# A two-part convolution, attention and expert kernel: three more rounds of expert weights and three token pieces are loaded before the first part ends

## The chip, the cores and the metric

One Trainium2 chip, one of its cores. The metric is the time of one execution on the device in microseconds (us); lower is better. All tensors are float32.

## The reference

The input is 8 images of 128 channels and 56 x 56 points (3136 points, called tokens later).

1. Deformable convolution: the group-normalised image gives 18 offsets a point; nine taps are gathered at the shifted places, weighted, and multiplied by `conv_w`; the input is added.
2. Attention: each image's 3136 tokens are normalised, then causal attention with one head of 128, added to the tokens (`t2` below).
3. Experts, which the change is about. Cut to what matters:

```python
logits = einsum('bsd,ed->bse', x, gate_w) + gate_b        # x: normalised tokens, 64 experts
probs = softmax(logits, axis=1)                            # over the tokens
topv, topi = the 8 largest tokens of each expert
pooled = sum over the 8 of topv * x[topi]                  # [8 images, 64 experts, 128]
h = gelu([pooled, 1] @ weight1[e])                         # 129 x 512 for each expert
out = [h, 1] @ weight2[e]                                  # 513 x 128 for each expert
outputs[topi] += out * topv
```

## The kernel before, in words

The kernel is two programs, one after the other, each of five engines that wait for each other by semaphores; a barrier of all engines stands between them.

**First part** (`first_part`, L328). It goes through 8 x 25 = 200 tiles of 128 tokens (`ALL` = 200), as a pipeline of steps written out by hand: in step `s` tile `s` is sampled and convolved, tile `s - 6` gets its scores, tile `s - 7` its probabilities and attention, tile `s - 8` (`LAG_T` = 8) its result `t2`, which SP stores four tiles at a time in `t2_dram` (L525). Small work (`MISC`) is hung on the steps: the logits of the gate (L669), and, 9 to 14 steps into the next image, the eight largest logits, the exponentials, the sparse probabilities (`logit` after that), the sum `rz`, and `pooled` (L921). SP stores the probabilities in `pm_dram` (L544, semaphore `pm_out`) and the sums in `rz_dram` (L545, semaphore `rz_out`). For the last image there are no more tiles beside this: steps 200 to 214 only finish it. This stretch is called the drain.

SP's queue runs in program order, its waits included. On it are the stores, the token loads, and the first expert weights: round 0 in the seventh image, rounds 1 to 3 at step `ALL + 1`, once the last convolution is done, because `shared`, where these weights go, holds the padded image and the gathered taps until then. At the end SP waits for the three late loads, for all stores of probabilities and sums, and for the token stores; then comes the barrier.

**Second part** (`second_part`, L1297). 64 experts in 16 rounds of four (`ROUNDS` = 16, `EXPERTS` = 4). A round needs 1024 KB of first weights and 1024 KB of second weights, in a ring of four slots (`WSLOTS`) in `shared`. Beside it the token pieces: each image's `t2` comes back from `t2_dram` in two pieces (16 in all, by POOL into three `stage` buffers), is turned by TensorE (L1543, seven units of up to 512 tokens an image) and kept in `res`, 8 x 3136 columns, by VectorE (even units, L1455) and ScalarE (odd units, L1425).

TensorE's order for each `k` from 0 to 18 is: first product of round `k` (L1507); placing of the outputs of round `k - 3` (L1552); the first two units of piece `k`; the turning of round `k - 1`'s hidden values (L1516); the rest of the units; second product of round `k - 2` (L1527). SP's order for each `k` is: wait until round `k - 2`'s first product frees the slot, load the first weights of round `k + 2`; wait for round `k - 4`'s second product, load the second weights of round `k`. POOL loads piece `k` when piece `k - 3` has been turned.

When all rounds are placed, VectorE scales the outputs by `rz` (L1486), TensorE multiplies them with the stored probabilities (L1584, 56 products, seven or eight banks ahead), VectorE adds each to `res` (L1496), and ScalarE's queue stores `res` in 16 pieces (12.85 MB). The probabilities of the first two images come through the `stage` buffers, of the others through `shared`.

## Time and profile before

| what | value |
|---|---|
| three runs | 2759.89, 2761.46, 2781.64 us |
| median | 2761.46 us |
| the profiled execution, its time | 2761.01 us |
| the profiled execution, its span | 2759.0 us |
| mean granted clock of TensorE | 0.975 of full |
| TensorE busy | 2556.5 us, 93% of the span |
| DMA, mean over the span | 139 GB/s |

The span is the time from the first to the last recorded event of the profiled execution; the execution's own time is 2.0 us longer. The shares are means over both parts, which differ: the first part ends near 2609 us, and the second takes the remaining 150 us. Times below count from the span's start. "SPq", "POOLq" and "ACTq" are the queues on which these engines issue DMAs; the time of such a row is that of the issue, not of the transfer.

### The profile page before, as it was taken

To read this page: it belongs to the slowest core of one execution; us is meant where nothing else is said; L and a number is where in the kernel's file an instruction comes from. 1 tells how busy PE (TensorE), PEld (TensorE's weight loads), DVE (VectorE), ACT (ScalarE), POOL (GpSimd) and SP (SyncE) were. 2 spreads that over 40 slices of the span, in tenths; PEclk is the share of its full clock that TensorE was granted. 3 is DMA by queue.
4 is the path that set the end of the run, shared out by engine and by line. 5 is a ranking of instruction groups with operands and counts; after the bars stand their busy time and mean duration, and the time that the engine had idled before them with its cause. 6 is when DMAs were issued, how large, how long until landed. Compare 5 with 4: busy or idle time off the path is not lost. (4 is left out here: it accounts for less than half of the span.)

```text
span 2759.0 us, 53901 instructions
## 1 busy us (share of the span) xinstructions
PE 2556.5 (93%) x19262; PEld 2042.3 (74%) x19262; DVE 1890.7 (69%) x7300; ACT 1777.5 (64%) x4144; POOL 1768.3 (64%) x1831
## 2 busy tenths in 40 slices
PE   4688999999999999999999999999999998999687
PEld 3466787777877787778877787778877887777564
DVE  4457767876687766876687777867688767765435
ACT  3456767667776767766776767666776767665330
POOL 4777776777577766777577766777577766740000
PEclk8799999999999999999999999999999999999899
DMA  6354434643356334643266334734364333432299
GB/s 188 112 159 135 117 113 128 159 131 113 91 168 148 115 104 127 162 121 113 87 176 146 113 101 130 173 108 121 92 165 150 112 103 111 120 80 96 68 397 395
DMA packets 218150, 382.63 MB, mean 139 GB/s; under 512 B 43786, under 2 KB 128714, under 8 KB 216988
## 3 DMA queue, kind: packets, MB, share of 16 engines
q0 software_dynamic: 88992, 250.76, 32.3%
q1 hardware_dynamic: 126299, 113.98, 13.9%
q10 hardware_dynamic: 2592, 14.45, 1.3%
q8 instruction: 154, 2.52, 0.4%
q14 instruction: 113, 0.92, 0.1%
HBM read 316.92 MB, written 62.13 MB: 137 GB/s over the span
## 5 line engine op out<-in xcount | busy, mean ns | idle before, releaser
L592 POOL DMA_INDIRECT shared<-pair_table,idx x1800 | 1747.8, 971 | 700.1 <-issue 537.0
L1250 PEld LDWEIGHTS bank_o<-vals,prob_t 128*128 128x128 f32 x4800 | 584.5, 192 | 120.6 <-ACT prob_t L639 65.0
L1250 PE MATMUL bank_o<-vals,prob_t 128*128 128x128 f32 x4800 | 613.0, 277 | 35.9 <-ACT prob_t L639 35.9
L639 ACT ACTIVATE prob_t<-bank_r 128x512 f32<-128x512 f32 (+2 forms) x704 | 369.6, 546 | 415.7 <-PE bank_r L1236 414.0
L889 DVE SCALAR_TENSOR_TENSOR shared<-shared,wb 128x128 f32<-128x128 f32 x1800 | 514.8, 347 | 167.9 <-ACT shared L620 166.8
L901 DVE CUSTOM_DVE_ANT_0 prob<-bank_r,mask 128x512 f32<-128x512 f32 (+2 forms) x704 | 429.0, 624 | 249.3 <-PE bank_r L1227 231.0
L620 ACT ACTIVATE shared<-shared,wa 128x128 f32<-128x128 f32 x1800 | 560.3, 391 | 60.1 <-DMA shared<-pair_table,idx 59.0
L1227 PE MATMUL bank_r<-keys,qt 128*128 128x512 f32 (+3 forms) x1344 | 587.9, 554 | 0.7 <-ACT qt L662 0.3
L1209 PE MATMUL bank_r<-convw_t,smp_t 128*128 128x128 f32 x3600 | 478.5, 279 | 8.7 <-ACT smp_t L625 8.7
L1209 PEld LDWEIGHTS bank_r<-convw_t,smp_t 128*128 128x128 f32 x3600 | 443.6, 195 | 49.6 <-ACT smp_t L625 28.0
L1236 PE MATMUL bank_r<-ident,prob 128*128 128x128 f32 x2504 | 367.0, 273 | 4.1 <-ACT prob L721 3.9
L1227 PEld LDWEIGHTS bank_r<-keys,qt 128*128 128x128 f32 x1344 | 228.7, 193 | 143.5 <-issue 141.1
L721 ACT ACTIVATE prob<-prob,nmax 128x1664 f32<-128x1664 f32 (+23 forms) x200 | 325.3, 1626 | 13.8 <-DVE nmax L1019 12.5
L1201 PE MATMUL bank_r<-ident,shared 128*128 128x128 f32 x1800 | 262.0, 286 | 73.1 <-DVE shared L889 73.0
L1236 PEld LDWEIGHTS bank_r<-ident,prob 128*128 128x128 f32 x2504 | 291.8, 141 | 19.2 <-issue 12.7
L1201 PEld LDWEIGHTS bank_r<-ident,shared 128*128 128x128 f32 x1800 | 208.8, 146 | 109.3 <-DVE shared L889 99.0
L625 ACT ACTIVATE smp_t<-bank_r 128x384 f32<-128x384 f32 x600 | 248.8, 484 | 11.8 <-PE bank_r L1201 10.9
L1005 DVE TENSOR_TENSOR t<-bank_r,t 128x128 f32<-128x128 f32 x200 | 57.1, 286 | 154.1 <-PE bank_r L1209 154.1
L934 DVE SCALAR_TENSOR_TENSOR t<-bank_o,inv_total,t 128x128 f32<-128x128 f32 x192 | 67.3, 350 | 51.4 <-PE bank_o L1250 39.8
L1370 POOL MEMSET pooled_t<- 128x1024 f32 x1 | 1.0, 952 | 151.5 <-POOLq L330 151.5
L1111 PE MATMUL bank_r<-shared,offw_t 128*32 128x448 f32 x896 | 98.0, 554 | 0.0
L1132 PEld LDWEIGHTS bank_r<-wv_t,keys 128*128 128x128 f32 x400 | 54.7, 197 | 29.5 <-issue 29.5
(189 smaller groups left out, 2260.2 us busy)
## 6 DMA issues: line engine op xcount, KB each, us to landing
shared<-in_dram SPq DMA_DIRECT2D x32, 1024.0 KB, 17.9
shared<-pair_table,idx POOLq DMA_INDIRECT x1800
pair_table<-rows_out SPq DMA_DIRECT2D x112, 256.0 KB
t<-in_dram SPq DMA_DIRECT2D x48, 256.0 KB
t_dram<-t SPq DMA_DIRECT2D x48, 256.0 KB
shared<-in_dram SPq DMA_DIRECT2D x7, 1568.0 KB, 14.8
stage<-t_dram POOLq DMA_DIRECT2D x8, 832.0 KB, 7.4
pm_dram<-logit SPq DMA_DIRECT2D x8, 800.0 KB, 6.6
```

Source lines behind the costliest of these rows:

```text
L592: pool.indirect_dma_start(g[t % RING][:, n, :], None, pair_table[b % 2], bass.IndirectOffsetOnAxis(ap=idx[:, b % 2, i * TAPS + n:i * TAPS ...
L620: last = act.activation(first, first, ACT.Copy, scale=wa[:, b % 2, i * TAPS + n:i * TAPS + n + 1])
L625: act.activation(smp_t[p][:], ring_bank(("smp", t, p))[:, 0:3 * P], ACT.Copy).then_inc(smp_ev, 1)
L639: act.activation(prob_t[q % 3][:, 0:w], ring_bank(("prob", t, c))[:, 0:w], ACT.Copy)\
L721: act.activation(row, row, ACT.Exp, bias=nmax[r][:, 0:1], accum_out=total[r][:, 0:1])\
L889: last = dve.scalar_tensor_tensor(first, g[t % RING][:, n, C:], wb[:, b % 2, i * TAPS + n:i * TAPS + n + 1], first, ALU.mult, ALU.add)
L901: dve.tensor_tensor_reduce(prob_at(t, k0, w), ring_bank(("score", t, c))[:, 0:w], m, 1.0, NEG, ALU.add, ALU.max, cmax[t % 2][:, c:c + 1]). ...
L1201: last = pe.transpose(bank[:, n * P:(n + 1) * P], g[step % RING][:, 3 * p + n, 0:C], ident[:])
L1209: last = pe.matmul(ring_bank(("conv", step, 0))[:, 0:P], smp_t[p][:, n % 3 * P:(n % 3 + 1) * P], convw_t[:, n, :], start=(n == 0), stop=(n ...
L1227: last = pe.matmul(bank[:, 0:w], qt[k % 2][:, at:at + P], key_chunk(tb, k0, w), start=True, stop=True)
L1236: last = pe.transpose(ring_bank(use)[:, n * P:(n + 1) * P], prob_at(v, k0 + n * P, P), ident[:])
L1250: last = pe.matmul(attn_ps, prob_t[q % 3][:, n * P:(n + 1) * P], vals[:, slot(tb, at), :], start=(at == 0), stop=(at == ti))
```

## The change

The large buffers of the second part, `res` and the three `stage` buffers, are now allocated before the first part, and most of the first part's tiles (`prob`, `t1`, `rows_out`, `xf`, `logit`, `keys`, `vals` in `res`; `convw_t`, `qt`, `prob_t`, `xf_t`, two of `smp_t` in `stages`) are cut out of them. Before, both parts' tiles lay over each other by the allocator's choice.

Three more weight slots lie in `res`: two where `keys` and `vals` are, one over `t1`, `rows_out` and the end of `prob`. Round 0 uses the last of the seven; rounds 1 to 4 use the four of `shared` and are loaded where 0 to 3 were; rounds 5 and 6 use the other two. Rounds 0, 5 and 6 are loaded by SP at step `ALL + LAG_T`, when the last attention is done and the last `t2` is made. From round 7 on the ring is the four slots of `shared`.

POOL loads token pieces 0, 1 and 2 at the end of its first part: when the last convolution and attention are done, and the third also when the last logits have been multiplied.

SP no longer waits at the end of the first part for the late loads, the probabilities and the sums. In the second part ScalarE waits for `pm_out` ahead of its first copy, VectorE for `late_in` and `pm_out`, POOL and SP for `pm_out` ahead of their loads of probabilities, and SP waits for `rz_out` at `k` = 7 and loads the sums there.

```diff
-EXPERTS, WSLOTS = 4, 4
+EXPERTS, WSLOTS, MORE_SLOTS = 4, 4, 3
+STAGES = 3
 WHALF = EXPERTS * HID
 NEG = -3.0e38
 EPS = 1e-5
 RSQRT_GUESS = float(0x5f3759df)
 MIDDLE = 12 * P
 PROB_COLS = 48 * P
+STAGE_COLS = NP - GPI // 2 * CHUNK
+MORE_AT = [B * N - 4 * WHALF, B * N - 2 * WHALF, PROB_COLS + T1_GROUPS * PER * C + 2 * ROW_GROUP * C - 2 * WHALF]
+FIRST_LOADS = WSLOTS + MORE_SLOTS
 END = ALL + 16
 
 
@@ -301,23 +305,47 @@
...
+def expert_slots(shared, res):
 
     halves = [shared[:, h * WHALF:(h + 1) * WHALF] for h in range(2 * WSLOTS)]
+    halves += [res[:, at + h * WHALF:at + (h + 1) * WHALF] for at in MORE_AT for h in range(2)]
     return ([h.rearrange("p (e h) -> p e h", e=EXPERTS) for h in halves[0::2]],
...
-def load_experts(sp, k, which, w1, w2, shared, w_in):
-
-    r, at = k % WSLOTS, slice(k * EXPERTS, (k + 1) * EXPERTS)
-    w1s, w2s = expert_slots(shared)
+def expert_slot(k):
+
+    if k == 0:
+        return FIRST_LOADS - 1
+    return k - 1 if k < FIRST_LOADS else (k - FIRST_LOADS) % WSLOTS
+
+
+def loads_of_slot(k):
+
+    return sum(expert_slot(u) == expert_slot(k) for u in range(k + 1))
+
+
+def slot_user_before(k):
+
+    return max(u for u in range(k) if expert_slot(u) == expert_slot(k))
+
...
+def load_experts(sp, k, which, w1, w2, slots, w_in):
+
+    r, at = expert_slot(k), slice(k * EXPERTS, (k + 1) * EXPERTS)
+    w1s, w2s = slots
...
+def load_stage(pool, k, stage, t2_dram, stage_in):
+
+    b, h = divmod(k, 2)
+    n0, n1 = (0, GPI // 2 * PER) if h == 0 else (GPI // 2 * PER, TILES)
+    pool.dma_start(stage[k % STAGES][:, 0:(n1 - n0) * C].rearrange("p (t c) -> p t c", c=C),
+                   t2_dram[b][:, n0:n1, :]).then_inc(stage_in[k % STAGES], 16)
...
+        stage = [stages[:, r * STAGE_COLS:(r + 1) * STAGE_COLS] for r in range(STAGES)]
+        at_res, at_stages = [0], [0]
+
+        def part(of, at, cols):
+            at[0] += cols
+            return of[:, at[0] - cols:at[0]]
...
-        convw_t = sb("convw_t", [P, TAPS, P])
+        convw_t = part(stages, at_stages, TAPS * P).rearrange("p (n o) -> p n o", o=P)
...
-        smp_t = [sb(f"smp_t{p}", [P, 3 * P]) for p in range(PIECES)]
-        rows_out = [sb(f"rows_out{r}", [P, ROW_GROUP, C]) for r in range(2)]
-        t1 = sb("t1", [P, T1_GROUPS * PER, C])
         bn_a, mv_a = sb("bn_a", [P, 6]), sb("mv_a", [P, T1_GROUPS * PER, 2])
...
-        keys = sb("keys", [P, SLOTS * P])
-        vals = sb("vals", [P, SLOTS, P])
-        qt = [sb(f"qt{r}", [P, CHUNK]) for r in range(2)]
-        prob = sb("prob", [P, PROB_COLS])
+        prob = part(res, at_res, PROB_COLS)
+        t1 = part(res, at_res, T1_GROUPS * PER * C).rearrange("p (s c) -> p s c", c=C)
+        rows_out = [part(res, at_res, ROW_GROUP * C).rearrange("p (i c) -> p i c", c=C) for r in range(2)]
+        assert MORE_AT[2] >= MIDDLE + N and MORE_AT[2] + 2 * WHALF == at_res[0]
+        xf = part(res, at_res, SLOTS * C).rearrange("p (s c) -> p s c", c=C)
+        logit = part(res, at_res, NP)[0:E, :]
+        smp_t = [part(of, at, 3 * P) for of, at in ((res, at_res), (stages, at_stages), (stages, at_stages))]
+        keys = part(res, at_res, SLOTS * P)
+        vals = part(res, at_res, SLOTS * P).rearrange("p (s c) -> p s c", c=P)
+        assert at_res[0] == B * N and B * N - 2 * SLOTS * P == MORE_AT[0]
+        qt = [part(stages, at_stages, CHUNK) for r in range(2)]
+        prob_t = [part(stages, at_stages, CHUNK) for r in range(3)]
+        xf_t = part(stages, at_stages, CHUNK)
+        assert at_stages[0] <= STAGES * STAGE_COLS
...
+                if step == ALL + LAG_T:
+
+                    after(attended, ALL)
+                    after(t2_done, ALL)
+                    for k in (0, WSLOTS + 1, WSLOTS + 2):
+                        for which in (1, 2):
+                            load_experts(sp, k, which, w1, w2, slots, w_in)
...
@@ -548,7 +599,7 @@
                     filled(after, ("chunk", B - 1, OFF_CHUNKS - 1))
                     after(rows_ev, ROW_GROUPS * B)
                     for which in (1, 2):
-                        load_experts(sp, 0, which, w1, w2, shared, w_in)
+                        load_experts(sp, 1, which, w1, w2, slots, w_in)
                 if step == (B - 1) * TILES + 20:
 
                     after(indexed, B)
@@ -558,12 +609,9 @@
                 if step == ALL + 1:
 
                     after(conv_done, ALL)
-                    for k in range(1, WSLOTS):
+                    for k in range(2, WSLOTS + 1):
                         for which in (1, 2):
-                            load_experts(sp, k, which, w1, w2, shared, w_in)
-            after(late_in, 16 * 3)
-            for done in (pm_out, rz_out):
-                after(done, 16 * B)
+                            load_experts(sp, k, which, w1, w2, slots, w_in)
...
+            for k in range(STAGES):
+
+                for r in range(2):
+                    after(t2_out[r], 16 * len(range(r, GPI * (k // 2 + 1), 2)))
+                after(conv_done, ALL)
+                after(attended, ALL)
+                if k == STAGES - 1:
+                    filled(after, ("logit", B - 1, GPI - 1))
+                load_stage(pool, k, stage, t2_dram, stage_in)
...
-        res = sb("res", [P, B, N])
-        w1s, w2s = expert_slots(shared)
-        stage = [sb(f"stage{r}", [P, NP - HALF * CHUNK]) for r in range(STAGES)]
+        res = res[:].rearrange("p (b n) -> p b n", n=N)
+        w1s, w2s = slots
+        stage = [stages[:, r * STAGE_COLS:(r + 1) * STAGE_COLS] for r in range(STAGES)]
...
-            for k in range(TURN_PIECES):
-                if k >= STAGES:
-                    pool.wait_ge(res_tp, units_of(k - STAGES)[-1] + 1)
-                b, h = divmod(k, 2)
-                n0, n1 = (0, HALF * PER) if h == 0 else (HALF * PER, TILES)
-                pool.dma_start(stage[k % STAGES][:, 0:(n1 - n0) * C].rearrange("p (t c) -> p t c", c=C),
-                               t2_dram[b][:, n0:n1, :]).then_inc(stage_in[k % STAGES], 16)
+            for k in range(STAGES, TURN_PIECES):
+                pool.wait_ge(res_tp, units_of(k - STAGES)[-1] + 1)
+                load_stage(pool, k, stage, t2_dram, stage_in)
+            pool.wait_ge(pm_out, 16 * B)
...
         @block.sync
         def _(sp):
-            for h in range(2):
-                sp.dma_start(rz[E * h:E * (h + 1), :], rz_dram.rearrange("(p h) e a -> h e (p a)", h=2)[h],
-                             allow_slow_non_contiguous=True).then_inc(small_in, 16)
             sp.dma_start(place[:], c_place).then_inc(place_in, 16)
-            for k in range(ROUNDS):
-                if WSLOTS <= k + 2 < ROUNDS:
-                    sp.wait_ge(first_mm, k + 2 - WSLOTS + 1)
-                    load_experts(sp, k + 2, 1, w1, w2, shared, w_in)
-                if k >= WSLOTS:
-                    sp.wait_ge(second_mm, k - WSLOTS + 1)
-                    load_experts(sp, k, 2, w1, w2, shared, w_in)
+            for k in range(FIRST_LOADS - 2, ROUNDS):
+                if k == FIRST_LOADS:
+                    sp.wait_ge(rz_out, 16 * B)
+                    for h in range(2):
+                        sp.dma_start(rz[E * h:E * (h + 1), :], rz_dram.rearrange("(p h) e a -> h e (p a)", h=2)[h],
+                                     allow_slow_non_contiguous=True).then_inc(small_in, 16)
+                if k + 2 < ROUNDS:
+                    sp.wait_ge(first_mm, slot_user_before(k + 2) + 1)
+                    load_experts(sp, k + 2, 1, w1, w2, slots, w_in)
+                if k >= FIRST_LOADS:
+                    sp.wait_ge(second_mm, slot_user_before(k) + 1)
+                    load_experts(sp, k, 2, w1, w2, slots, w_in)
+            sp.wait_ge(pm_out, 16 * B)
             for p in range(1, PAIRS):
-                sp.wait_ge(second_mm, ROUNDS - WSLOTS + p)
+                sp.wait_ge(second_mm, ROUNDS - PAIRS + p)
...
             act.wait_ge(padded, 3)
+            act.wait_ge(pm_out, 16 * B)
...
             dve.memset(pooled_t[:, E // 2:, :], 0.0).then_inc(padded_d, 1)
+            dve.wait_ge(late_in, 16 * 3)
+            dve.wait_ge(pm_out, 16 * B)
...
-                pe.wait_ge(w_in[0][k % WSLOTS], 16 * (k // WSLOTS + 1))
+                pe.wait_ge(w_in[0][expert_slot(k)], 16 * loads_of_slot(k))
```

## Rows read from the trace of the kernel before

**Rows 1.** The page's head: span and instructions.
```profile
span 2759.0 us, 53901 instructions
```
**Rows 2.** Busy table by stretches: stretch, length, busy of each engine, clock, DMA share, GB/s.
```profile
2500.00:2520.00 20.00, 20.00 (x129) 15.48 (x128) 10.71 (x41) 10.44 (x16) 0.00 (x0) 1.00 0.75 279
2520.00:2540.00 20.00, 20.00 (x140) 16.55 (x139) 9.71 (x41) 8.28 (x14) 0.00 (x0) 1.00 0.04 14
2580.00:2600.00 20.00, 8.53 (x81) 6.78 (x82) 14.42 (x42) 8.02 (x18) 0.00 (x0) 0.71 0.11 25
2640.00:2660.00 20.00, 16.91 (x190) 12.56 (x188) 5.11 (x20) 5.07 (x11) 1.58 (x3) 0.83 1.04 398
```
**Rows 3.** Chain of waits in the second part: start us, us, what.
```profile
2610.75 4.96 DMA stage<-t_dram
...
2632.45 21.93 DMA shared<-in_dram
...
2665.62 18.21 DMA shared<-in_dram
...
2690.27 20.25 DMA shared<-in_dram
...
2720.74 27.78 DVE res L1496 x51
```
**Rows 4.** DMA view of 2611 to 2710.5: totals, issues, median us to landing.
```profile
DMA packets 14946, 38.96 MB, mean 392 GB/s; under 512 B 922, under 2 KB 922, under 8 KB 14937
...
shared<-in_dram SPq DMA_DIRECT2D x24, 1024.0 KB, 18.1
stage<-t_dram POOLq DMA_DIRECT2D x8, 832.0 KB, 7.4
stage<-t_dram POOLq DMA_DIRECT2D x8, 768.0 KB, 7.6
```
**Rows 5.** DMA view of the whole second part, 2608.9 to 2759.
```profile
DMA packets 18700, 58.11 MB, mean 387 GB/s; under 512 B 1536, under 2 KB 1536, under 8 KB 18304
```
**Rows 6.** Timeline of the drain: start us, us, engine, line, operation; a SPq row is an issue.
```profile
2577.95 6.13 SPq L525 DMA_DIRECT2D t_dram<-t  x2
...
2587.77 0.31 ACT L669 ACTIVATE logit<-bank_r,gate_bias 64x64 f32<-64x64 f32 x1 [0.42 <-PE bank_r L1145]
...
2597.66 0.47 SPq L544 DMA_DIRECT2D pm_dram<-logit  x1
2598.18 0.60 SPq L545 DMA_DIRECT2D rz_dram<-rz  x1
...
2604.38 0.22 DVE L921 COPY pooled<-bank_r 128x64 f32<-128x64 f32 x1 [0.53 <-PE bank_r L1160]
```
**Rows 7.** Timeline of POOL in the second part: its first memset, its fourth piece.
```profile
2608.93 0.95 POOL L1370 MEMSET pooled_t<- 128x1024 f32 x1 [151.45 <-POOLq L330]
...
2619.13 0.53 POOL L1379 DMA_DIRECT2D stage<-t_dram  x1 [6.72 <-PE bank_q L1543]
```
**Rows 8.** DMA view of 2582 to 2612: the last stores, us to landing.
```profile
pm_dram<-logit SPq DMA_DIRECT2D x1, 800.0 KB, 5.6
...
rz_dram<-rz SPq DMA_DIRECT2D x1, 0.2 KB, 10.2
```
**Rows 9.** SP's six weight issues at the end of the tiles: the first and the last.
```profile
2496.15 0.39 SPq L322 DMA_DIRECT2D shared<-in_dram  x1
...
2500.88 2.51 SPq L324 DMA_DIRECT2D shared<-in_dram  x1
```
**Rows 10.** Timeline of TensorE, rounds 0 and 1.
```profile
2611.34 1.94 PE L1507 MATMUL bank_h<-shared,pooled_t 128*32 128x512 f32 x8 [7.01 <-ACT pooled_t L1409]
2615.76 3.08 PE L1543 MATMUL bank_q<-ident,stage 128*128 128x128 f32 x12 [2.48 <-DMA stage<-t_dram]
2618.76 1.16 PE L1507 MATMUL bank_h<-shared,pooled_t 128*32 128x512 f32 x8
```
**Rows 11.** Timeline of TensorE: rounds 4 and 5 begin, round 7 ends.
```profile
2631.35 1.04 PE L1507 MATMUL bank_h<-shared,pooled_t 128*32 128x512 f32 x8
...
2636.25 1.04 PE L1507 MATMUL bank_h<-shared,pooled_t 128*32 128x512 f32 x8
...
2650.26 1.08 PE L1527 MATMUL both_y<-shared,act_h 128*32 128x128 f32 x32
```
**Rows 12.** Timeline of the tail: output scale, last addition.
```profile
2718.90 1.13 DVE L1486 SCALAR_TENSOR_TENSOR shared<-bank_of_outputs,rz_all,shared 128x128 f32<-128x128 f32 x4 [1.25 <-PE bank_of_outputs L1552]
...
2750.37 0.21 DVE L1496 TENSOR_TENSOR res<-both_y,res 128x64 f32<-128x64 f32 x1
```

More of the change, by code:

```diff
@@ L303, in hybrid_kernel @@
         shared = ctx.enter_context(nc.sbuf_tensor("shared", [P, WSLOTS * 2 * WHALF], F32))
-        w_in = [[ctx.enter_context(nc.semaphore(f"w{which}_in{r}")) for r in range(WSLOTS)] for which in (1, 2)]
-        first_part(nc, x_cm, x_tok, off_w, off_b, conv_w, wq, wk, wv, gate_w, gate_b, w1, w2, base, b1_t, b2, pooled, ident, shared, w_in,
+        res = ctx.enter_context(nc.sbuf_tensor("res", [P, B * N], F32))
+        stages = ctx.enter_context(nc.sbuf_tensor("stages", [P, STAGES * STAGE_COLS], F32))
@@ new lines, in hybrid_kernel @@
+        slots = expert_slots(shared, res)
+        w_in = [[ctx.enter_context(nc.semaphore(f"w{which}_in{r}")) for r in range(WSLOTS + MORE_SLOTS)] for which in (1, 2)]
+        stage_in = [ctx.enter_context(nc.semaphore(f"stage_in{r}")) for r in range(STAGES)]
+        rz = ctx.enter_context(nc.sbuf_tensor("rz", [P, 1], F32))
+        pm_out, rz_out, late_in = (ctx.enter_context(nc.semaphore(n)) for n in ("pm_out", "rz_out", "late_in"))
+        first_part(nc, x_cm, x_tok, off_w, off_b, conv_w, wq, wk, wv, gate_w, gate_b, w1, w2, base, b1_t, b2, pooled, ident, shared, res, stages, slots, w_in, stage_in, rz, pm_out, rz_out, late_in,
@@ L306, in hybrid_kernel @@
                    c_base, c_ident, c_mask, c_group, pair_table, t2_dram, pm_dram, rz_dram)
-        second_part(nc, w1, w2, b1_t, b2, pooled, ident, shared, w_in, t2_dram, pm_dram, rz_dram, c_place, out)
-def expert_slots(shared):
+        second_part(nc, w1, w2, b1_t, b2, pooled, ident, shared, res, stages, slots, w_in, stage_in, pm_out, rz_out, late_in, t2_dram, pm_dram, rz_dram, c_place, out)
+def expert_slots(shared, res):
     halves = [shared[:, h * WHALF:(h + 1) * WHALF] for h in range(2 * WSLOTS)]
+    halves += [res[:, at + h * WHALF:at + (h + 1) * WHALF] for at in MORE_AT for h in range(2)]
@@ L421, in first_part @@
         t2_out = [sem(f"t2_out{r}") for r in range(2)]
-        pm_out, rz_out = sem("pm_out"), sem("rz_out")
         stats_done, affine_done, normalised, indexed = (
@@ L1294, in _, with second_part @@
                     fill_misc(use)
-def second_part(nc, w1, w2, b1_t, b2, pooled, ident, shared, w_in, t2_dram, pm_dram, rz_dram, c_place, out):
+def second_part(nc, w1, w2, b1_t, b2, pooled, ident, shared, res, stages, slots, w_in, stage_in, pm_out, rz_out, late_in, t2_dram, pm_dram, rz_dram, c_place, out):
     G = EXPERTS
-    STAGES = 3
     J = HID // P
@@ L1348, in second_part @@
         padded, padded_d = sem("padded"), sem("padded_d")
-        stage_in = [sem(f"stage_in{r}") for r in range(STAGES)]
         first_mm, first_ev = sem("first_mm"), sem("first_ev")
@@ L1507, in first @@
                     last = pe.matmul(bank_h[k % 2][COLS * g:COLS * (g + 1), :], pooled_t[:, k * G + g, :],
-                                     w1s[k % WSLOTS][:, g, :], start=True, stop=True)
+                                     w1s[expert_slot(k)][:, g, :], start=True, stop=True)
                 last.then_inc(first_mm, 1)
```

17 lines of the change are left out of this document (6 added, 11 removed).

## The prediction

> **What bounds the kernel now.** The page comes first: span 2759.0 us [rows 1], in a run of 2761.01 us, so 2.0 us lie outside the span, and that run is 0.45 us under the median of 2761.46. The change works at the seam of the two parts, so I read the busy table by stretches next [rows 2]. It shows three regimes. Up to 2580 TensorE is full (20.00 of 20 us). From 2580 to 2608.9 the last image drains: TensorE 8.53 of 20, DMA share 0.11, 25 GB/s. From 2609 on the DMA share is 1.04 at 398 GB/s. The chain of waits over the second part agrees: its long pieces are expert weights in flight (21.93, 18.21 and 20.25 us), then VectorE's last adds [rows 3]. A load of 1024 KB takes 2.7 us at 392 GB/s, so 20 us is time spent in a full queue.
>
> So the second part is bound by bytes. The DMA view from its first stage issue to the last weight wait gives 38.96 MB at a mean of 392 GB/s, with 24 weight loads of 1024 KB and 16 token pieces of 768 or 832 KB [rows 4]. The whole second part moves 58.11 MB [rows 5].
>
> The drain is a chain of small steps: the last token tile is stored at 2583.8 (SP row ends 2584.08), the last logits are kept at 2587.8, SP stores the probabilities at 2597.66 and the sums at 2598.18, and `pooled` is complete at 2604.60 [rows 6]. Then nothing computes until 2608.93, where POOL's memset opens the second part [rows 7]: the store of the sums takes 10.2 us to land (2598.18 + 10.2 = 2608.4), and SP waits for it before the barrier [rows 8].
>
> **The change part by part.**
> 1. Bytes moved into the drain. Rounds 0, 5 and 6 are six loads of 1024 KB; three token pieces are 768 + 832 + 768 KB. Together 8512 KB = 8.72 MB. At 392 GB/s [rows 4] they are worth 22.2 us of the second part. By the Trainium skill ("DMA: Bandwidth & Descriptors", Specifications), HBM gives one core about 358 GB/s; the estimate by that page would be 24.3 us. The 392 measured here decides.
> 2. Do they fit? POOL's first two pieces can go when attention ends (about 2582.3), SP's loads from 2584.1 on; the third piece waits for the last logits at 2587.8 [rows 6]. 8.72 MB take 22.2 us, so they end near 2606.5 if they start at about 2584. The drain lasts until 2604.6. They fit but for 2 us. Round 0's weights used to be loaded hundreds of microseconds earlier, beside a full TensorE; now they are in this batch, and I count them.
> 3. Does the traffic slow the drain's engines? Six such loads ran from 2496.15 to about 2514 [rows 9] while TensorE stayed at 20.00 of 20 us in that stretch and in the next [rows 2]. I take nothing. The bound above is half again on the 20.9 us from 2583.7 to 2604.6, 10 us; below is nothing.
> 4. SP's wait for the two stores leaves the end of the first part. The second part then opens at `pooled`, 2604.6, plus the 0.5 us that lay between the landing and the memset: 2605.1 against 2608.93, 3.8 us sooner. SP must be through by then. Its six issues took 2496.15 to 2503.4 [rows 9]; the same from 2584.1 ends by 2591.4, before the store at 2597.66.
> 5. New waits: ScalarE and VectorE wait for `pm_out` at the head of the second part. Queued behind are ScalarE's copies of the first product and of the odd token units and VectorE's copies of the even units; TensorE waits for the copies from its third unit on, and POOL's next piece waits for TensorE. The store of the probabilities landed 5.6 us after its issue [rows 8]; now it stands on SP's queue behind six loads. If it passed them, it would land at 2603.3 and cost nothing. If it goes behind them, (8.72 + 0.82) MB from 2584 on take 24.3 us, plus 1.6 us for completion: 2610. I take the latter, since loads on that queue took some 20 us to land behind others [rows 3]. The Trainium skill ("DMA: Bandwidth & Descriptors", Queues, rings and completion order) says that each DMA engine consumes a ring's descriptors in order; by that rule too the store stays behind. Upper end: it lands as late after its turn as the sums did, 2608.4 + 10.2 = 2618.6.
> 6. Start of the second part. Before: first product 2611.34, tokens wait for their piece until 2615.76, three units take 3.08 us, so round 0 ends at 2618.8 [rows 10]. After: product at 2611.34 - 3.8 = 2607.5, 1.94 us long, then three units at once, 3.08 us: 2612.6, which is 6.2 us sooner. The third unit starts at 2611.5 and needs a copy of 0.69 us after `pm_out`: 2610 + 0.7 is just in time; each microsecond beyond 2610.8 delays all of it.
> 7. When do the DMA engines fill up again? Before, the first piece was issued at 2610.75 [rows 3]. After, the three pieces are there, and the next issue is piece 3, at 2619.13 [rows 7] - 6.2 = 2612.9. The saturated stretch begins 2.2 us later.
> 8. Does it stay saturated? From 2612.9 to 2639.3 TensorE's order releases pieces 3 to 8 (4.9 MB) and six weight halves (first weights of rounds 7 to 10, second weights of 7 and 8: 6.3 MB), 11.2 MB. From 2614.3 on, 25.0 us serve 9.8 MB. 1.4 MB are left at the thinnest point, so it doesn't run dry; then round 11's first weights and the rest follow at 2.9 MB per round of 5.0 us [rows 11], 580 GB/s, more than can be served. For thin places I take 1 us off. SP's wait for `rz_out` stands ahead of two loads due at 2621; the sums need to land by then, and even a lag of 10.2 us after 2608.4 gives 2618.6.
> 9. TensorE: rounds 1 to 7 end at 2651.34 now [rows 11], 2645.1 then; eight more at 5.0 us give 2685.1. From the second product that ends round 15 to VectorE's output scale are 8.3 us now (2710.56 by [rows 3]: 2690.27 + 20.25, to 2718.90 [rows 12]), so free-running TensorE would reach that scale at 2692.4, 26.5 us sooner. That is more than the bytes allow, so bytes stay the bound.
> 10. The tail (stores of 12.85 MB and VectorE's 56 adds, 2718.90 to 2750.58, then the last store [rows 12]) isn't changed and moves as a whole. Both it and the transfers fill it.
> 11. The layout of the first part's tiles, the semaphores' places and the changed slot numbers issue nothing: 0. The place load and the sums' loads are the same bytes.
>
> Sum: 22.2 - 2.2 - 1.0 = 19.0 us. 2761.0 - 19.0 = **2742.0 us**, 0.7% less.
>
> **The rivals.**
> - A, the store of the probabilities is late and takes the place of the wait that was removed. At 2618.6 the third unit starts at 2619.3, not 2611.5: 7.8 us lost, gain 11.2, 2749.8. For: it is behind 6.3 MB, and the store of the sums shows that 10 us for a landing happens. Against: it landed in 5.6 us itself. Chance 0.16.
> - B, TensorE becomes the bound: it starts after a pause at half clock (the product of round 0 took 1.94 us, that of a later round 1.04 [rows 10, 11]). If three rounds ran so, it would lose 3 x 4 = 12 us, scale at 2704.4, gain 14.5, 2746.5. Against: by 2618.8 the length was nearly 1.04 again. Chance 0.10.
> - C, the transfers are quicker than 392 GB/s beside less competition, and TensorE's chain is the bound: gain 26.5, 2734.5. Chance 0.08.
> - D, slower than before: the tiles' new places in `res` and `stages` cost the first part. It has 200 tile steps in 2496 us, 12.5 each [rows 9]. 0.1 us on each is 20 us, at which the gain is gone; 0.24 is 48, and the kernel is at 2790. No row shows that a place matters; nothing excludes it. Chance 0.05.
> - E, nothing comes: the drain stretches by 10 us and the second part starts thin. Within 5 us of before. Chance 0.05.
> - The forecast, 2737 to 2747: 0.56.
>
> **The range.** A measurement of this kernel can tell about 1% (27.6 us) from no change. The range takes the forecast, A, B and the upper part of C: 2736 to 2752 holds 0.8 and more. To be over 1% faster takes 2733.8, beyond C: 0.05. Slower by over 1% is the far part of D: 0.03. Within 1%: 0.92.
>
> **What would show it.** The barrier at 2605 by the old clock, not 2609 (step 4). The store of the probabilities landing about 12 us after its issue (step 5). DMA share near 1 from 2584 to 2606, then a hole of some 5 us, then near 1 to the end, with no second hole before 2640 (steps 2, 7, 8). VectorE's output scale about 20 us earlier (step 9). Second part's bytes 49.4 MB instead of 58.11. Wrong would make it: a drain longer than 21 us from the last token store to `pooled`; units waiting for ScalarE or VectorE until after 2612; or the first part up to 2580 ending later by microseconds (D).

## The result and the profile after

| | before | changed |
|---|---|---|
| seven runs each, median | 2763.84 us | 2748.19 us |
| lowest to highest | 2759.89 to 2781.64 | 2744.98 to 2755.24 |
| ratio, 95% interval | | 0.9932 [0.9906, 0.9957] |
| span of the profiled execution | 2759.0 us | 2744.5 us |

The changed kernel is 0.68% faster. The same kernel was timed a second time later, against another set of runs of the kernel before: 2748.16 us, ratio 0.9953 [0.9933, 0.9972]. The two spans differ by 14.5 us, and a second profile of the changed kernel has 2745.2 us, so the gain is 14 us in the profiles and 13 to 19 by the ratios; a few microseconds of 2750 are beyond what the times can tell. The forecast was 19.0 us and 2742.0 us. The median lies inside the range of 2736 to 2752, but outside the 2737 to 2747 that the forecast proper was given: it is 6.2 us above the forecast and 1.6 us under the 2749.8 of rival A (the store of the probabilities is late).

The changed kernel's busy table by stretches, columns as in [rows 2]:

```profile
span 2744.5 us, 53906 instructions
```

```profile
2585.00:2606.77 21.77, 10.35 (x80) 8.92 (x80) 10.99 (x27) 6.86 (x16) 0.53 (x1) 0.61 1.02 386
2606.77:2617.00 10.23, 4.89 (x24) 2.52 (x28) 1.86 (x3) 2.16 (x3) 1.88 (x3) 0.77 0.41 149
2617.00:2650.00 33.00, 32.72 (x400) 24.25 (x396) 12.26 (x46) 14.06 (x28) 4.11 (x8) 0.97 0.98 358
```

The drain now has a DMA share of 1.02 at 386 GB/s where it had 0.11 at 25 [rows 2]. Behind it lies a hole: 10.2 us with a share of 0.41. Then the transfers run on, in the first 33 us at a mean of 358 GB/s instead of 392.

What happens at the seam is in the timeline of the changed kernel (SP's and POOL's issues and TensorE's work, put in order of time):

```profile
2578.50 6.14 SPq L569 DMA_DIRECT2D t_dram<-t  x2
2584.69 0.43 SPq L350 DMA_DIRECT2D res<-in_dram  x1
...
2594.47 2.49 SPq L352 DMA_DIRECT2D res<-in_dram  x1
2598.21 1.38 SPq L595 DMA_DIRECT2D pm_dram<-res  x1
...
2599.53 5.81 PE L1212 MATMUL bank_r<-res 128*64 128x128 f32 x50 [0.69 <-ACT res L731]
...
2606.77 0.95 POOL L1425 MEMSET pooled_t<- 128x1024 f32 x1 [17.39 <-POOLq L366]
...
2609.19 1.93 PE L1565 MATMUL bank_h<-res,pooled_t 128*32 128x512 f32 x8 [2.97 <-ACT pooled_t L1464]
2611.05 1.71 PE L1601 MATMUL bank_q<-ident,stages 128*128 128x128 f32 x8
...
2615.68 1.02 PE L1601 MATMUL bank_q<-ident,stages 128*128 128x128 f32 x4 [2.92 <-DVE res L1513]
...
2617.01 0.53 POOL L360 DMA_DIRECT2D stages<-t_dram  x1 [8.36 <-PE bank_q L1601]
```

The barrier opens at 2606.77, the first two units are turned by 2612.76, and then the third waits 2.92 us for VectorE's copy of the first. VectorE waits for the store of the probabilities, as the DMA view of 2560 to 2615 (last column: us to landing) and the chain of waits say:

```profile
pm_dram<-res SPq DMA_DIRECT2D x1, 800.0 KB, 16.6
```

```profile
2598.21 16.55 DMA pm_dram<-res
2614.85 0.70 DVE res L1513
...
2672.21 19.09 DMA shared<-in_dram
...
2705.89 27.77 DVE res L1554 x51
```

This store took 5.6 us before [rows 8]. Between these pieces the chain is TensorE's rounds, with hardly a gap from 2622 to 2670, and then one last weight load; before it was weight loads for most of the way [rows 3]. VectorE's output scale comes 14.8 us sooner than in [rows 12], and what follows it is about as long as before (40.4 us, 40.1 before):

```profile
2704.06 1.12 DVE L1544 SCALAR_TENSOR_TENSOR shared<-bank_of_outputs,rz_all,shared 128x128 f32<-128x128 f32 x4 [1.25 <-PE bank_of_outputs L1610]
```

### The profile page after: what moved, and what is told of

Read it like the earlier page. It is cut to its first block, busy times and chain, and to the rows that moved or that the text cites. A ratio compares the mean times of both kernels' runs of the same rounds, so it can differ in the third digit from the quotient of the medians.

```text
span 2744.5 us, 53906 instructions
## 1 busy us (share of the span) xinstructions
PE 2550.7 (93%) x19262; PEld 2037.1 (74%) x19262; DVE 1890.6 (69%) x7300; ACT 1778.3 (65%) x4144; POOL 1771.8 (65%) x1831
## 4 chain that ended last, share of the span: by engine, by line
PE 70%; ACT 10%; DVE 9%; POOL 5%; issue 3%; DMA 2%; SPq 0%; DVEq 0%; ACTq 0%; POOLq 0%
PE bank_r L1284 17%; PE bank_o L1307 16%; PE bank_r L1266 12%; PE bank_r L1293 9%; POOL shared L640 5%; PE bank_r L1258 5%; ACT shared L677 5%; DVE shared L946 3%; PE bank_r L1189 2%; PE bank_r L1168 1%; ACT stages L696 1%; ACT res L778 1%; DVE res L1554 1%; DVE res L1111 1%; PE bank_r L1281 1%
## 5 line engine op out<-in xcount | busy, mean ns | idle before, releaser
L1307 PEld LDWEIGHTS bank_o<-res,stages 128*128 128x128 f32 x4800 | 584.5, 192 | 121.7 <-ACT stages L696 66.3
L1307 PE MATMUL bank_o<-res,stages 128*128 128x128 f32 x4800 | 613.0, 277 | 37.0 <-ACT stages L696 37.0
L696 ACT ACTIVATE stages<-bank_r 128x512 f32<-128x512 f32 (+2 forms) x704 | 369.7, 546 | 418.6 <-PE bank_r L1293 416.9
L958 DVE CUSTOM_DVE_ANT_0 res<-bank_r,mask 128x512 f32<-128x512 f32 (+2 forms) x704 | 429.4, 624 | 250.0 <-PE bank_r L1284 231.7
L1284 PE MATMUL bank_r<-res,stages 128*128 128x512 f32 (+3 forms) x1344 | 587.7, 554 | 0.7 <-ACT stages L719 0.3
L1293 PE MATMUL bank_r<-ident,res 128*128 128x128 f32 x2504 | 366.9, 273 | 4.1 <-ACT res L778 4.1
L1266 PE MATMUL bank_r<-stages 128*128 128x128 f32 x2400 | 335.6, 277 | 0.0
L778 ACT ACTIVATE res<-res,nmax 128x1664 f32<-128x1664 f32 (+23 forms) x200 | 325.2, 1626 | 13.9 <-DVE nmax L1076 12.5
L1293 PEld LDWEIGHTS bank_r<-ident,res 128*128 128x128 f32 x2504 | 291.7, 141 | 19.2 <-issue 12.7
L1266 PEld LDWEIGHTS bank_r<-stages 128*128 128x128 f32 x2400 | 302.9, 194 | 0.0
```

Of the source, the lines that this page charges most:

```text
L696: act.activation(prob_t[q % 3][:, 0:w], ring_bank(("prob", t, c))[:, 0:w], ACT.Copy)\
L778: act.activation(row, row, ACT.Exp, bias=nmax[r][:, 0:1], accum_out=total[r][:, 0:1])\
L958: dve.tensor_tensor_reduce(prob_at(t, k0, w), ring_bank(("score", t, c))[:, 0:w], m, 1.0, NEG, ALU.add, ALU.max, cmax[t % 2][:, c:c + 1]). ...
L1266: last = pe.matmul(ring_bank(("conv", step, 0))[:, 0:P], smp_t[p][:, n % 3 * P:(n % 3 + 1) * P], convw_t[:, n, :], start=(n == 0), stop=(n ...
L1284: last = pe.matmul(bank[:, 0:w], qt[k % 2][:, at:at + P], key_chunk(tb, k0, w), start=True, stop=True)
L1293: last = pe.transpose(ring_bank(use)[:, n * P:(n + 1) * P], prob_at(v, k0 + n * P, P), ident[:])
```

## How the experiments are compared

The differences sought are 1 to 5 us of 2750, less than the times can tell. The profiles can, if one thing is taken out: the last tiles end at different times, in eleven of the twelve runs below at 2576.4 to 2580.6 and in one at 2587.4 (2577.95 before). So all runs are read from a **mark**, the start of SP's issue of the token store of the last full group (first row above), to the end of the span. "Piece 3" is POOL's first token load behind the barrier's hole, the moment from which the second part's transfers are asked for again. The last column is the ratio of the times to the kernel before, with 95% intervals that reach 0.002 to 0.003 to either side; the kernels e5, e7 and e12 have none, they were executed only once, in the profile. e7's mark is 8 us later than the others', at a mean granted clock of 0.971 instead of 0.973 to 0.979; its two added transfers are issued 19 us after the mark, so they are not the reason.

| kernel | landing of probabilities, us from issue | barrier, us from mark | third unit held, us | piece 3, us from mark | end, us from mark | time against before |
|---|---|---|---|---|---|---|
| before | 5.6 | 31.0 | | | 181.1 | |
| changed | 16.6 | 28.3 | 2.9 | 38.5 | 166.0 | 0.9932 |
| changed, second profile | 17.2 | 27.0 | 5.9 | 39.2 | 165.9 | 0.9953 |
| e1 stores on POOL | 12.1 | 37.6 | 0 | 45.2 | 170.6 | 0.9988 |
| e2 round 6 behind the store | 12.6 | 26.9 | 1.3 | 34.6 | 161.6 | 0.9938 |
| e3 weights only | 12.9 | 28.0 | 0 | 40.0 | 167.2 | 0.9961 |
| e4 SP's wait kept | 17.2 | 37.7 | 0 | 45.2 | 170.6 | 0.9958 |
| e5 one round | 5.6 | 26.9 | 0 | 41.9 | 173.3 | |
| e7 two more ahead | 16.6 | 27.9 | 7.3 | 42.9 | 169.6 | |
| e9 sums in SBUF | 13.0 | 28.1 | 0 | 35.9 | 161.2 | 0.9926 |
| e10 and round 6 behind | 7.7 | 26.9 | 0 | 33.6 | 158.8 | 0.9921 |
| e10 again | 7.6 | 27.0 | 0 | 33.6 | 158.8 | 0.9916 |
| e11 eight slots | 7.8 | 27.0 | 0 | 33.6 | 159.0 | 0.9946 |
| e12 pieces late | 5.7 | 27.0 | 0 | 37.3 | 162.8 | |

In e3, e5 and e12 the units wait for the pieces themselves, not for a copy.

## The experiments

**The wait put back (e4).** SP waits again at the end of the first part:

```diff
+            for done in (pm_out, rz_out):
+                after(done, 16 * B)
             for r in range(2):
                 after(t2_out[r], 16 * len(range(r, B * GPI, 2)))
```

> SP's wait for the last image's two stores stands at the end of the first part again; all loads stay in the drain. The store of the sums landed at about 2615.0 in the changed kernel, so the barrier opens near 2615.5 instead of 2606.8. Theory 1: first product near 2617.9, round 0 ends near 2623 instead of 2616.7, and everything moves by it: span 2750 to 2751. Theory 3 (slack in the bytes absorbs a late start): within 2 us of 2744.5.

The barrier opened 9.4 us later after the mark, piece 3 went out 6.7 us later, the end came 4.6 us later than in the changed kernel (time against the kernel before: 0.9958 [0.9930, 0.9985]). The forecast was a loss of 5.5 to 6.5 us. Two microseconds of the 6.7 are absorbed, but not all: the start does gate the end. The removed wait is worth 4.6 us beside the loads; the 3.8 us of my step 4 was of the right kind. What removing the wait gives without the loads was not tried.

**Two more transfers ahead of the store (e7).** The same question with a dose. The two transfers are copies of 1024 KB within memory that nobody reads:

```diff
+                    for h in range(2):
+                        sp.dma_start(spare_dram[h], w2[4 * h:4 * h + 4, 0:HID, :].rearrange("e (p j) o -> p e (j o)", p=P)).then_inc(spare_in, 16)
```

> The changed kernel with two more transfers of 1024 KB on SP's queue ahead of the last image's stores (from the weights into a spare tensor in memory, used by nobody). They take at least 5.4 us at 392 GB/s, so the probabilities land 22 us or more after their issue. Theory 1 (this landing gates the start one for one): the third unit is held 5.4 us longer, and the end comes at 171 us or more after the mark. Theory 3 (slack in bytes absorbs it): 166 to 167.5 us.

The store still took 16.6 us from its issue, but SP could issue it only at 2611.37, 24.0 us after the mark instead of 19.7, because it was still busy with the issues ahead (the timeline of SP in this kernel):

```profile
2605.97 5.30 SPq L594 DMA_DIRECT2D spare_dram<-in_dram  x2
2611.37 2.60 SPq L599 DMA_DIRECT2D pm_dram<-res  x1
```

From the mark the landing is 4.3 us later, the third unit is held 7.3 us instead of 2.9, piece 3 goes out 4.4 us later, and the end comes 3.6 us later. So the landing at 22 us or more from the issue did not come, and the end of 169.6 lies between the two theories (171 or more, 166 to 167.5). The 5.4 us were too large for the delay, but the end follows the landing nearly one for one (3.6 of 4.3 us, in one execution).

**Fewer loads ahead of the store (e2).** SP issues round 6's two loads behind the last image's stores:

```diff
-                    for k in (0, WSLOTS + 1, WSLOTS + 2):
+                    for k in (0, WSLOTS + 1):
...
                         sp.dma_start(rz_dram[b - 1], rz[0:E, :]).then_inc(rz_out, 16)
+                        if b == B:
+                            for which in (1, 2):
+                                load_experts(sp, WSLOTS + 2, which, w1, w2, slots, w_in)
```

> SP issues round 6's two loads behind the last image's two stores instead of ahead of them; same bytes in the drain. Theory 1: with two loads fewer ahead, (4.19 + 2.42 + 0.82) MB at 392 GB/s are 19.0 us from 2585, so the store's data are out at 2604 and it lands by 2608; no wait of the third unit, span 2741.6. Theory 2: landing 14 us or more after issue, span 2744.5. Theory 3: no wait, span within 1 us of 2744.5.

It landed in 12.6 us instead of 16.6, the unit waited 1.3 us, and the end came 4.4 us sooner. The barrier opened 1.4 us sooner, because the 50 pooling matmuls ran 4.40 us and not 5.81, but that is no part of the gain: the second profile of the changed kernel has the barrier as early (27.0) and ends no sooner (165.9). Theory 1 holds for the end. But 12.6 is more than the 9.7 us that I had worked out from the bytes ahead, and the busy table of this kernel has a strange stretch:

```profile
2606.00:2612.00 6.00, 2.88 (x17) 1.67 (x18) 1.33 (x2) 2.15 (x3) 1.32 (x3) 0.77 0.93 143
```

A DMA share of 0.93 and 143 GB/s: the engines count as busy and move little. This was not in my forecast.

**The stores on POOL's queue (e1).** The last image's two stores are issued by POOL, with semaphores of their own:

```diff
+            after(chosen, len(SHARES) * B)
+            after(rz_done, B)
+            pool.dma_start(pm_dram[B - 1], logit[:]).then_inc(LATE["pm"], 16)
+            pool.dma_start(rz_dram[B - 1], rz[0:E, :]).then_inc(LATE["rz"], 16)
```

> Only the queue of the last image's two stores changes: POOL issues them instead of SP, so they do not stand behind the six weight loads. Theory 1 (my forecast was too high by the late store of the probabilities, which landed 16.6 us after its issue behind six loads and held the third token unit for 2.9 us): the store lands within about 8 us, the third unit does not wait for it, POOL's piece 3 is issued some 2.9 us sooner after the barrier than in the changed kernel (10.2 us after it there), and the span is 2741.6 against 2744.5. Theory 2 (any store lands late while the DMA engines are full, whatever its queue): it still lands 14 to 17 us after its issue and the span stays at 2744.5. Theory 3 (the missing microseconds are the slower pooled product and a thin supply, the wait costs nothing because the bytes absorb it): the wait goes and the span stays within 1 us of 2744.5.

None of the three theories. The store passed the loads only in part (12.1 us), and the barrier opened 11 us after `pooled` (POOL's timeline):

```profile
2600.90 0.56 POOL L658 DMA_DIRECT2D rz_dram<-rz  x1
2617.81 0.94 POOL L1431 MEMSET pooled_t<- 128x1024 f32 x1 [16.35 <-POOLq L368]
```

By the times the kernel is no faster than before that can be told (0.9988 [0.9966, 1.0009]); from the mark its profile ends 10.5 us sooner than before and 4.6 later than the changed kernel. Every engine's last computation ended by 2606.8, and POOL is the only one that was given more to do at the end, so POOL was probably the last to reach the barrier; no row shows it. Both stores had landed by 2613.3, 4.5 us before the barrier, and the last of SP's weight loads landed at 2617.4, 0.4 us before it. Whether POOL waited for that load is open; in the changed kernel the barrier opened while such loads were still on their way. These loads crept here too: 148 GB/s from 2610 to 2614.

**Only the weights in the drain (e3).** The pieces are loaded behind the barrier, as before the change.

```diff
-            for k in range(STAGES):
-
-                for r in range(2):
...
-                load_stage(pool, k, stage, t2_dram, stage_in)
...
-            for k in range(STAGES, TURN_PIECES):
-                pool.wait_ge(res_tp, units_of(k - STAGES)[-1] + 1)
+            for k in range(TURN_PIECES):
+                if k >= STAGES:
+                    pool.wait_ge(res_tp, units_of(k - STAGES)[-1] + 1)
                 load_stage(pool, k, stage, t2_dram, stage_in)
```

> The three token pieces are loaded after the barrier again, as before the change; the three rounds of weights stay in the drain. Second part's bytes rise by 2.42 MB, worth 6.2 us at 392 GB/s. Theory 1 (the second part is set by bytes and by when its DMA engines fill up): the pieces fill the hole that the changed kernel has from the barrier to its piece 3 (10 us), the store of the probabilities lands earlier, and the span is 2742 to 2745, as with the pieces in the drain. Rival (bytes moved into the drain are worth their transfer time whatever they are): 2744.5 + 6.2 = 2750.7.

The span is 2744.4 us, as theory 1 had it. From the mark it is 1.2 us worse than the changed kernel, though 2.42 MB more lie behind the barrier. The three pieces, 28% of the bytes that the change moves into the drain, are worth 1.2 us and not 6.2: they took up engines ahead of the store (it lands 12.9 us from its issue without them, 16.6 with them), and left the hole behind.

**One round only (e5).** Rounds 5 and 6 and the pieces behind the barrier, round 0 in the drain.

```diff
-                    for k in (0, WSLOTS + 1, WSLOTS + 2):
+                    for k in (0,):
...
             sp.dma_start(place[:], c_place).then_inc(place_in, 16)
+            for k in (WSLOTS + 1, WSLOTS + 2):
+                for which in (1, 2):
+                    load_experts(sp, k, which, w1, w2, slots, w_in)
```

> Layout, slots and waits of the changed kernel, but only round 0 is loaded in the drain; rounds 5 and 6 and the three token pieces are loaded right behind the barrier. Second part's bytes are those of the kernel before less 2.10 MB. Theory: 5.4 us for the bytes and 3 us for the earlier barrier, so the end comes 181.1 - 8.4 = 172.7 us after the mark, and the mark itself lies within 3 us of 2578.0. Rival (the new layout slows the first part): the mark lies 5 us or more later.

173.3 us against 172.7 expected: 5.4 us for 2.10 MB and 3 for the barrier is about right, and the mark at 2576.4 is no later than before; all this in one execution. This run has the clearest rows for the strange stretch. The barrier opened at 2603.25, and pieces and weights were issued at once, but the store of the sums was still on its way (busy table; DMA view):

```profile
2604.00:2608.00 4.00, 1.07 (x8) 0.16 (x8) 0.44 (x1) 1.67 (x2) 2.73 (x6) 0.88 1.05 50
2608.00:2612.00 4.00, 0.00 (x0) 0.00 (x0) 0.00 (x0) 0.00 (x0) 0.00 (x0) 0.50 0.92 352
```

```profile
rz_dram<-rz SPq DMA_DIRECT2D x1, 0.2 KB, 10.5
```

Issued at 2596.60, it landed at 2607.1. Up to 2608 the transfers move 50 GB/s at a mean share of 1.05, and from then on 352. The mean hides something: by single microseconds the share is 2.72, then 0.51, 0.57 and 0.38, so after the first one the engines are not all busy, and still next to nothing is moved. e3 has the same: its pieces are issued at 2607.10, the sums land at 2610.2, and the transfers move 56 GB/s from 2607 to 2610 and 330 in the three microseconds after. Before the change nobody wanted to transfer anything while the sums were on their way, so the only sign was a landing of 10.2 us for 256 bytes [rows 8]. The Trainium skill ("DMA: Bandwidth & Descriptors", Specifications) has transfers below 512 bytes done as read-modify-write and off line rate; these are 64 writes of 4 bytes. The rows here agree that they are far off the rate (10.5 us for 256 bytes); that others are held up by them is what these rows show, and by what mechanism they do not.

**The sums kept in SBUF (e9).** So the next kernel takes the single words away, their store in the first part and their load in the second:

```diff
-                        sp.dma_start(rz_dram[b - 1], rz[0:E, :]).then_inc(rz_out, 16)
...
                         dve.tensor_copy(rz[E:, :], rz[0:E, :]).then_inc(rz_done, 1)
+                        after(rz_done, b)
+                        at_h, at_p = E * ((b - 1) % 2), (b - 1) // 2
+                        link(dve.tensor_copy(KEPT["rz"][at_h:at_h + E, at_p:at_p + 1], rz[at_h:at_h + E, :]))
```

> The sums never go through memory: VectorE copies them into rz_all in SBUF at once, so there is no store of 64 single words behind the store of the probabilities, and no load of them. Since the ends of the first part differ from run to run by up to 3 us, I count from SP's issue of the token store of the last full group (2578.5 in the changed kernel, whose span ends 166.0 us later; in the kernel before 181.1 us later). Theory 4 (the store of single words holds up what is in flight beside and behind it for some 5 us, the probabilities' completion among it): the probabilities land at most 12.5 us after their issue instead of 16.6, the third unit does not wait, and the end comes 163 us after the mark. Theory 1 (the six loads ahead are all of it): landing 16 us or more after issue, end 166 us after the mark.

Landing 13.0 us after the issue, a bit more than the 12.5 I set, and 3.6 less than with the words. The unit does not wait (TensorE's timeline: the three units in one row, no idle time):

```profile
2610.83 1.94 PE L1562 MATMUL bank_h<-res,pooled_t 128*32 128x512 f32 x8 [2.96 <-ACT pooled_t L1462]
2612.69 3.18 PE L1598 MATMUL bank_q<-ident,stages 128*128 128x128 f32 x12
```

The end comes 4.8 us sooner than in the changed kernel (expected 3); 2.6 us of it lie ahead of piece 3, 2.2 behind it. The load of the sums, which took 10.1 us to land in the changed kernel, is gone too, but it explains little of the 2.2: e4 has that load and needs 125.5 us from piece 3 to the end, e9 125.3, the changed kernel 127.5. About half a microsecond of it is TensorE's clock: behind the wait the first product of round 1 took 1.94 us, in e9 1.42. The load alone was not tried.

**Both (e10).** The sums in SBUF and round 6 behind the store.

> As the kernel with the sums in SBUF, and round 6's two loads are issued behind the store of the probabilities. With the single words in the way these two loads crept at some 140 GB/s from 2606 to 2612. Theory 4: they run at 380 GB/s or more, the probabilities land at most 9 us after their issue (12.6 with the words), no wait of the third unit, end 160 us after the mark (161.6 with the words). Theory 1 or a slow phase by another cause: the creeping stays, landing 12 us or more, end 161 to 162 us after the mark.

Landing 7.7 us, and the engines move what they are asked (busy table):

```profile
2608.00:2612.00 4.00, 2.57 (x16) 1.52 (x16) 0.74 (x2) 1.67 (x2) 0.90 (x2) 0.84 1.05 385
2612.00:2616.00 4.00, 3.88 (x25) 2.24 (x24) 1.04 (x3) 1.75 (x4) 0.53 (x1) 0.74 0.28 58
```

385 GB/s at a share of 1.05 from 27.9 us after the mark, where e2, from 27.4 us after it, had 143 at 0.93. The landings now form a ladder: 5.7 us with no backlog (e12), 7.7 with the pieces and two rounds ahead, 13.0 with the third round ahead too (2.10 MB at 392 GB/s are 5.35 us, the step is 5.3), 16.6 with the single words. Queue and words are separate, and both are shown by taking them away. The words delay the store of the probabilities only when loads are ahead of it: 16.6 against 13.0 us (e9) and 12.6 against 7.7 (e2, e10), but 5.6 with them and 5.7 without when nothing is ahead (e5, e12). The end is 7.2 us sooner than in the changed kernel.

**Its time (e0 and e10 again, on one chip).**

> The changed kernel once more, beside the next one on the same chip. Its profile shows how far one execution stands from another: the mark (SP's issue of the last full group's token store) within 2576 to 2581, the end 165 to 167 us after it, and the third token unit again held by the store of the probabilities for 2 to 4 us.

> The kernel with the sums in SBUF and round 6's loads behind the store once more, for its time beside the changed kernel: end 158 to 160 us after the mark, that is 7 us or 0.25% less than the changed kernel, and 0.8% less than the kernel before.

Changed: 2748.16 us, 0.9953 [0.9933, 0.9972]. With both edits: 2740.68 us, 0.9916 [0.9898, 0.9935] (and 0.9921 [0.9896, 0.9945] when it was first timed). The medians differ by 7.5 us, as the profiles do. In the second profile of the changed kernel the pooling matmuls took 4.49 us and the barrier opened 1.3 us sooner, and the third unit then waited 5.9 us instead of 2.9, more than the 2 to 4 that I expected: what TensorE wins ahead of the landing is lost at it.

**An eighth slot (e11).** To use the hole that is left (58 GB/s above), round 2 is loaded behind the barrier into the place of `xf`, and round 7 takes a slot in `shared`:

```diff
+    first = (6, 0, 7, 1, 2, 4, 5, 3)
+    return first[k] if k < len(first) else (k - len(first)) % WSLOTS
```

> As the last kernel, and an eighth weight slot where xf was: round 2 is loaded there right behind the barrier, into the hole in which the DMA engines wait for TensorE's first three units, and round 7 takes the slot in shared that is loaded at the end of the tiles. 2.10 MB less in the stretch that is set by bytes, 5.3 us at 392 GB/s. Theory (bytes and their hole set the end): 155 to 156 us after the mark, and 0.5% or more faster than the changed kernel. Rival (TensorE's rounds are the bound by now, at 5.0 us each): 159 to 160 us after the mark, as without the slot.

The hole is filled and the end doesn't move. The busy table of e11 comes first, then that of e10 for the later stretch:

```profile
2612.00:2616.00 4.00, 3.93 (x24) 2.33 (x25) 0.99 (x2) 1.85 (x4) 0.53 (x1) 0.73 1.05 386
...
2630.00:2650.00 20.00, 20.00 (x262) 15.52 (x260) 7.49 (x31) 7.17 (x15) 2.12 (x4) 1.00 0.94 338
```

```profile
2630.00:2650.00 20.00, 20.00 (x264) 15.38 (x262) 7.48 (x29) 7.18 (x15) 2.12 (x4) 1.00 1.03 397
```

386 instead of 58 GB/s early, 338 instead of 397 later, TensorE at 20.00 of 20 us in both. The slots of `shared` come free only as TensorE gets through its rounds, so bytes loaded earlier are bytes not asked for later. The rival was right: behind seven preloaded rounds TensorE's pace of 5.0 us a round is the bound of this stretch. The end hangs on one more thing: in both kernels the chain of waits leaves TensorE at 2676, where it frees the last slot, and the last weights land 20.3 us (e11) and 19.3 us (e10) later. By the times the eighth slot is no gain either: 2749.41 us in twelve executions, 0.9946 [0.9925, 0.9967], against 2740.61 in four of e10 beside it. Whether it costs something, the profile, which is one of e11's fastest executions, does not show.

**The pieces late, without words and queue (e12).**

> The same, but the three token pieces are loaded after the barrier. 2.42 MB more behind the barrier, 6.2 us at 392 GB/s; in that kernel the DMA engines wait some 4 us for TensorE's first units (58 GB/s from 2612 to 2616). Theory (a load behind the barrier costs nothing while it fills that hole, and a little for the later first units): end 159 to 161 us after the mark. Rival (pieces in the drain are worth their transfer): 165 us.

162.8, between the two, in one execution: the pieces in the drain are worth 4.0 us of their 6.2 here. TensorE's first units wait for piece 0 and start 3.5 us later after the mark than e10's (TensorE's timeline of e12):

```profile
2613.37 3.17 PE L1593 MATMUL bank_q<-ident,stages 128*128 128x128 f32 x12 [3.33 <-DMA stages<-t_dram]
```

## Why the prediction was right, and which steps were off

- **What bounds it, and the bytes (steps 1, 2, 10).** Right. Behind the barrier 50.54 MB are moved instead of 58.11; of these about 1 MB is the end of the drain's traffic. The drain took the rest in at 386 GB/s.

(DMA view of 2606.77 to the end:)

```profile
DMA packets 15431, 50.54 MB, mean 367 GB/s; under 512 B 1504, under 2 KB 1504, under 8 KB 14970
```

- **No cost to the drain's engines (step 3).** Mark to the last logits, exponentials and copies is the same to 0.1 us. The 50 pooling matmuls took 5.81 us, all of them at a granted clock of 0.50, and 4.49 in the second profile of the same kernel, where the granted clock was 1.00 for the last of them (from 2604 on). The same kernel with the same traffic runs them in either time, so the 1.3 us belong to the time at which the clock rose and not to the traffic.
- **The barrier (step 4).** 2605.1 forecast, 2606.77 measured: 0.55 the later mark, 1.33 those matmuls. In the second profile it is 27.0 us from the mark, 0.2 off the forecast. SP's six issues took 12.3 us (to 2596.96), not the 7.3 of my step, and were through only 1.3 us ahead of the store.
- **The store of the probabilities (step 5) is the term that was mis-sized.** I had it land at 2610, it landed at 2614.8. The place in the queue was right. I added 1.6 us for completion, which no row shows, and did not see that the 64 single words behind the store delay it, though their 10.2 us stood in [rows 8] and I used them only as an upper bound. In the changed kernel loads and data are through by 2611.2 (0.01 MB from 2613 to 2616), and only the landing is missing. Without the words (e9) the store lands 32.9 us after the mark, where my 2610 is 32.1; with them it is 36.3. A part of the 0.8 us may be that a store alone moves 202 to 211 GB/s (before, 2598 to 2602), not the 392 that I took for its 0.82 MB. The mechanism is rival A's, in a smaller size: A had the third unit start at 2619.3 instead of 2611.5, and it started at 2615.68 and 2617.15.
- **Start and saturation (steps 6, 7).** Round 0 ends 4.1 us later than forecast for these two reasons, and piece 3 goes out at 2617.01, not 2612.9. So the saturated stretch begins 6.3 us later than before, not 2.2.
- **Thin supply (step 8).** No dry spot, but 358 GB/s from 2617 to 2650. I took 1 us; 22.2 - 6.3 = 15.9, and 14.5 came, so 1.4 us are left for it (the later mark is in the 6.3).
- **The bound (step 9).** The scale came 14.8 us sooner, at what the bytes allow. But the chain runs over TensorE's rounds until 2670 and only then over a last weight load. My numbers had the two bounds 7.5 us apart (19.0 and 26.5 us of gain); here they are nearly equal, and in e11 taking 2.10 MB out of the stretch no longer helps. That bytes "stay the bound" was too strong.
- **Rivals.** A (the late store) is the cause of most of what is missing. B (half clock in the rounds) shows only in the first two rounds (first products of 1.93 and 1.94 us, 1.07 in the third); that its 14.5 us of gain and its scale at 2704.4 are nearly the measured ones is chance. C and E didn't come. D: nothing like 20 us. The eleven marks average 2579.3 against 2577.95 in the one profile of before, so a cost of the layout of a microsecond is not excluded, and not shown either.

The forecast by the sum is 19.0 us, the profiles have 14.5 and 13.8. Of the 4.5 us between, 4.1 are the later piece 3, that is steps 4 and 5 with 0.55 for the later mark; the other 0.4 are the thin supply. That the median still fell into the range is owed to the width that the rivals gave it, not to the sum.

## What to carry to other kernels

When transfers are moved into a quiet stretch, look at what small stores leave in it, and issue the bulk behind them in the same queue: a store of 800 KB took 5.6 us to land with nothing ahead, 16.6 behind six loads and beside single words. Keep single words out of memory if SBUF can hold them. And filling a hole in the DMA engines' time only pays while the consumer frees buffers faster than they can be filled.

## What the runs showed of the hardware

- Sixty-four writes of 4 bytes to memory take 10.2 to 10.5 us to land with nothing but one store ahead (before, e5), and 12.4 to 15.9 beside or behind the loads. While they are on their way, other transfers move at 50 GB/s (e5), 56 (e3) and 143 to 148 (e2, and e1, where POOL issues the words). The DMA share is 0.93 in e2; in e5 it is 2.72 in the first microsecond and 0.4 to 0.6 after. Without the words such a stretch has 385 GB/s (e10). With nothing else to move they leave the DMA share at 0.00 (before, 2603 to 2608). By what mechanism they hold the others is open.
- Of six issues of 1024 KB loads in a row on SP's queue the first three (four in e3, where no pieces are loaded beside them) take 0.4 to 1.2 us each, the later ones 2.3 to 4.9 us (changed, e0, e3). A store behind them on SP is issued late as well, by 4.3 us in e7.
- A store of 800 KB to memory with nothing beside it moves 202 to 211 GB/s at a DMA share near 1 (before, 2598 to 2602); loads move 386 to 392.
- With the last two stores issued by POOL just ahead of the barrier, it opened 4.5 us after they had landed and 0.4 us after the last weight load (e1). The cause was not found.
